# A mixture-of-experts block on one core: GpSimd's scatters in one run per round, results turned behind the third up step

## The chip, the cores and the metric

The kernel runs on one core of a Trainium2 chip. The metric is the device time of one execution in microseconds (us), the median of several runs. All tensors are float32 but for small bf16 tables of counts.

## The reference

The input is a batch of 8 images of 64 channels and 16 x 16 points, so 2048 tokens of 64 channels. First comes an attention over the 256 points of each image, then a feed-forward layer with 8 experts, of which each token uses the two with the largest logits.

```python
x = x + conv_attention(layernorm_over_channels(x))   # kq (32), v (32), softmax over 256 points, out (64)
t = tokens(x)                                        # 2048 x 64
n = layernorm(t)
gates = top2(softmax(n @ router_w.T)), renormalised  # 2 of 8 experts
h = silu(n @ w1[e].T) * (n @ w3[e].T)                # 682 hidden units
t = t + sum over the two experts of gate * (h @ w2[e].T)
```

## The kernel before

**First half.** The 2048 tokens lie as 16 tiles of 128. Two images (four tiles) are a pair, and the four pairs are worked through attention, layernorm and routing one after the other. Each token of a pair gets its two row numbers in a table `xs` in HBM, which holds a region of 2048 rows per expert. GpSimd writes the rows there by indirect DMAs: `scatter_row(p, at)` (from L354) sends one 128-row piece, `at` running over 4 tiles x 2 experts = 8 per pair, 32 in all. A row holds the 64 normalised channels and the number of its (token, expert) place.

**Second half.** The rows of the experts are cut into 39 pieces of 128 rows, which the code calls slots. Four slots are a round, so there are ten rounds (`NQ`), the last of three slots. Which expert a slot belongs to is computed on VectorE in three phases (after pair 1, pair 2 and pair 3), from which SyncE loads registers. The rows of rounds 0 and 1 need pairs 0 and 1, those of rounds 2 and 3 need pair 2, and those of rounds 4 to 9 need pair 3; SyncE waits for the scatters of these pairs (`landed(p)`, L299) ahead of `load_rows` (L292). `load_weights` (L276) loads the 565 KB of each slot's expert, with three rounds' worth of buffers. It waits for the down step of three rounds before.

A round i goes so:

- VectorE: `pair_up(i)` doubles the loaded rows (L781) and copies their place numbers to `y_row` (L786, L789). It stands on VectorE behind round i - 2.
- TensorE: `turn_x(i)` (L1013) transposes them into X_BANK, ScalarE's `columns(i)` (L496) copies them to `x_cols`.
- Six up steps s = 0 to 5. Step s of round i is number g = 6i + s. TensorE's `up(g)` makes 4 slots x 2 matmuls (L1031 with w1 in the upper half of the array, L1033 with w3 in the lower half); step 5 is the short tail (L1037). It signals `h1_done` and `h3_done`. ScalarE's `silu(g)` (L504, tail L508) and VectorE's `multiply(g)` (L827, tail L830) make the hidden units `hid`. TensorE may be one step ahead of silu and two ahead of multiply.
- TensorE's `down(i)` (L1059) multiplies `hid` by w2, 24 matmuls into one bank. ScalarE's `y_copy(i)` (L517) copies the result to SBUF, TensorE's `turn_y(i)` (L1073) transposes it back, VectorE's `results(i)` (L839) copies it to `y_out`, a ring of four rounds.
- GpSimd's `scatter_result(j)` (from L366) sends slot j's 128 rows of results by one indirect DMA to the table `ys` in HBM, in the order of (token, expert). It waits for `y_out_ready` at the first slot of a round.

TensorE's list of a round is up step 0, `turn_x(i+1)`, `turn_y(i-1)`, up steps 1 to 5, `down(i)`. VectorE's has `results(i-1)` behind `multiply` of step 0. No scheduler moves anything; each engine does its list in the order of the code, and the engines meet by semaphores.

**End.** When all results have landed, `ys` is read back in four parts, weighted by the gates, added to the tokens on TensorE, copied and stored.

GpSimd's own list, behind the tables of the start, is all row scatters, pair by pair, with the layernorm's inverse deviations in between, and then all result scatters:

```python
for p in range(PAIRS):
    for at in range(TPP * K_TOP):
        ...
        scatter_row(p, at)
...
for j in range(NS):
    scatter_result(j)
```

Of the kernel before, what the change touches and what calls it, by code (L numbers as in the profile page):

```python
# [16 lines left out]
K_TOP = 2  # L17
# [7 lines left out]
PAIRS = B // 2  # L25
TPP = 2 * TPB
# [5 lines left out]
QUAD = 4  # L32
CAP = B * N
NS = E + (K_TOP * CAP - 1) // SUB
NQ = -(-NS // QUAD)
# [16 lines left out]
STEPS = CHUNKS  # L52
# [9 lines left out]
def metaformer(nc, x_tok, projections, value_output, experts, xs, ys, out):  # L62
    with ExitStack() as ctx:
# [3 lines left out]
        def sem(name):  # L67
            return ctx.enter_context(nc.semaphore(name))
# [132 lines left out]
        h1_done, h3_done = sem("h1_done"), sem("h3_done")  # L201
# [124 lines left out]
        def _(pool):  # L326
# [38 lines left out]
            def scatter_result(j):  # L365
                i, h = divmod(j, QUAD)  # L366
                if h == 0:
                    pool.wait_ge(y_out_ready, i + 1)
                    pool.wait_ge(y_row_ready, i + 1)
                nc.gpsimd.indirect_dma_start(  # L370
                    ys, bass.IndirectOffsetOnAxis(ap=y_row[:, j:j + 1], axis=0),
                    y_out[:, i % RING, h, :], None).then_inc(y_scattered[i % RING], 16)
# [33 lines left out]
            pool.wait_ge(tables_made, TABLES)  # L406

            t_deviation(0)
            for p in range(PAIRS):
                for at in range(TPP * K_TOP):  # L410
                    if p == 0 and at == TPP * K_TOP - 2 or p == 2 and at == K_TOP:
                        t_deviation(p + 1)
                    scatter_row(p, at)
                if p == 1:
                    t_deviation(2)
            for j in range(NS):
                scatter_result(j)

        @block.scalar
# [128 lines left out]
        def _(dve):  # L548
# [306 lines left out]
            for i in range(NQ):  # L855
                for s in range(STEPS):
                    multiply(STEPS * i + s)
                    if s == 0 and i >= 1:
                        results(i - 1)
                    tables_between(i, s)  # L860
                if i + 2 < NQ:
                    pair_up(i + 2)
# [11 lines left out]
        def _(pe):  # L874
# [205 lines left out]
            for i in range(NQ):  # L1080
                for s in range(STEPS):
                    up(STEPS * i + s)
                    if s == (1 if i == 0 else 0) and i + 1 < NQ:
                        turn_x(i + 1)
                    if s == 0 and i >= 1:
                        turn_y(i - 1)
                down(i)
            turn_y(NQ - 1)
# [59 lines left out]
```

## Time and profile before

| what | value |
|---|---|
| timed runs | 174.99, 176.17, 176.45 us; median 176.17 |
| profiled execution, its span | 238.2 us |
| mean granted TensorE clock in it | 0.799 |
| TensorE busy (matmuls) | 166.9 us, 70% |
| VectorE busy | 99.7 us, 42% |
| GpSimd busy | 85.7 us, 36% |
| ScalarE busy | 70.8 us, 30% |
| result scatters on GpSimd (L370) | 39, 960 ns each |
| row scatters on GpSimd (L361) | 32, 987 ns each |
| first and last up step | from 68.5 us to 213.6 us of the span |

The profile is one execution that the hardware profiler recorded instruction by instruction; nothing of it lies outside the span of 238.2 us. That span is 62.0 us longer than the median of the timed runs, which are not recorded. Times in the rows are us from the start of the span. "Idle before" is how long the engine stood before an instruction, and the name behind the arrow is what ended that; "remote" is a release that the profile can't trace to an engine of this core, and "issue" stands where nothing that it shows was waited for.

### The profile page before, as it was taken

How to read it: one execution, taken by the hardware profiler on the slowest of the kernel's cores; microseconds unless marked ns; L12 is line 12 of the kernel's file. 1: busy time of each engine (PE TensorE's matmuls, PEld its weight loads, DVE VectorE, ACT ScalarE, POOL GpSimd, SP SyncE). 2: the span in 40 equal slices, each digit the busy share in tenths (PEclk: the TensorE clock that was granted, in tenths of full speed). 3: DMA queues.
4: the chain of work that ended last, by engine and by line, in shares of the span. 5: the costliest groups of instructions: out<-in, count | busy, mean ns of one | idle time of the engine just before them, and what ended most of it. 6: DMA issues, size and time to landing. Idle time of an engine off the chain costs nothing.

```text
span 238.2 us, 4880 instructions
## 1 busy us (share of the span) xinstructions
PE 166.9 (70%) x1682; PEld 139.1 (58%) x1682; DVE 99.7 (42%) x372; ACT 70.8 (30%) x141; POOL 85.7 (36%) x114
## 2 busy tenths in 40 slices
PE   3595957428683069589494994958949697895683
PEld 2364836307452068588393983948839597783543
DVE  2557568255583037584222433223232344342230
ACT  2377433013310034224232142222422323333101
POOL 2963577723277700603205033060230604142400
PEclk9999586555578559979799598895997979798579
DMA  6990000184570229652958075390661600000053
GB/s 185 322 297 20 11 25 22 31 267 151 159 290 23 50 81 328 216 210 46 364 169 313 3 240 196 88 346 4 203 228 42 266 10 14 11 15 11 17 176 91
DMA packets 19893, 33.00 MB, mean 139 GB/s; under 512 B 7691, under 2 KB 13100, under 8 KB 19868
## 3 DMA queue, kind: packets, MB, share of 16 engines
q1 hardware_dynamic: 16732, 29.55, 37.8%
q0 software_dynamic: 2272, 2.35, 3.0%
q10 hardware_dynamic: 864, 0.79, 1.0%
q8 instruction: 14, 0.23, 0.4%
q14 instruction: 11, 0.09, 0.1%
HBM read 25.55 MB, written 7.13 MB: 137 GB/s over the span
## 4 chain that ended last, share of the span: by engine, by line
issue 48%; POOL 21%; PE 11%; DVE 8%; DMA 3%; another core or an unknown queue 3%; ACT 3%; POOLq 1%; SPq 0%; ACTq 0%; DVEq 0%
POOL ys L370 15%; POOL xs L361 5%; PE psum L925 3%; PE psum L914 2%; ACT xn L426 2%; DMA y_in<-ys 2%; DVE rows L595 1%; PE psum L894 1%; PE psum L1103 1%; PE psum L885 1%; DMA ys<-y_out,y_row 1%; DMA proj<-projections 1%; DVE index L606 1%; DVE neg_max L584 1%
## 5 line engine op out<-in xcount | busy, mean ns | idle before, releaser
L370 POOL DMA_INDIRECT ys<-y_out,y_row x39 | 37.4, 960 | 104.0 <-DVE y_out L839 95.2
L827 DVE TENSOR_TENSOR hid<-psum,act_sb 128x512 f32<-128x512 f32 (+1 forms) x50 | 33.4, 676 | 88.9 <-ACT act_sb L504 61.6
L1031 PE MATMUL psum<-x_cols,weights 64*128 64x128 f32 x390 | 52.9, 286 | 13.9 <-issue 12.1
L1031 PEld LDWEIGHTS psum<-x_cols,weights 64*128 64x128 f32 x390 | 47.6, 193 | 19.4 <-issue 15.8
L1033 PE MATMUL psum<-x_cols,weights 64*128 64x128 f32 x390 | 53.1, 286 | 0.9 <-issue 0.9
L504 ACT ACTIVATE act_sb<-psum 128x512 f32<-128x512 f32 (+1 forms) x50 | 28.7, 586 | 70.0 <-remote 42.4
L1033 PEld LDWEIGHTS psum<-x_cols,weights 64*128 64x128 f32 x390 | 47.7, 193 | 1.1 <-issue 1.1
L1059 PE MATMUL psum<-hid,weights 128*64 128x128 f32 x468 | 42.8, 357 | 2.1 <-issue 1.1
L1059 PEld LDWEIGHTS psum<-hid,weights 128*64 128x64 f32 x468 | 39.3, 189 | 4.8 <-issue 2.7
L361 POOL DMA_INDIRECT xs<-xrows,pos x32 | 31.6, 987 | 12.9 <-issue 8.9
L1037 PE MATMUL psum<-x_cols,weights 64*106 64x128 f32 x78 | 8.7, 349 | 23.1 <-ACT act_sb L504 18.4
L1037 PEld LDWEIGHTS psum<-x_cols,weights 64*106 64x106 f32 x78 | 6.1, 208 | 24.7 <-ACT act_sb L504 19.6
L925 PE MATMUL psum<-u_sb,probsT 128*128 128x73 f32 x64 | 13.1, 373 | 5.2 <-issue 4.4
L925 PEld LDWEIGHTS psum<-u_sb,probsT 128*128 128x128 f32 x64 | 12.0, 281 | 7.6 <-issue 5.9
L517 ACT COPY y_cols<-psum 128x256 f32<-128x256 f32 (+1 forms) x10 | 3.6, 362 | 32.3 <-PE psum L1059 32.3
L957 PE MATMUL psum<-ones,before 128*128 128x512 bf16 x24 | 10.0, 562 | 1.8 <-issue 1.8
L452 ACT ACTIVATE probs<-psum,neg_max 128x256 f32<-128x256 f32 x16 | 6.7, 474 | 12.2 <-DVE neg_max L584 12.1
L460 ACT COPY probsT<-psum 128x512 f32<-128x512 f32 x8 | 4.7, 586 | 12.9 <-PE psum L914 8.5
L830 DVE TENSOR_TENSOR hid<-psum,act_sb 42x512 f32<-42x512 f32 x10 | 6.8, 682 | 3.5 <-ACT act_sb L508 3.5
L941 PE MATMUL psum<-taken,before 128*128 128x32 bf16 x4 | 0.7, 181 | 10.5 <-DVE taken L618 10.5
L914 PE MATMUL psum<-ident,probs 128*128 128x128 f32 x32 | 7.9, 395 | 0.3 <-ACT probs L452 0.3
L941 PEld LDWEIGHTS psum<-taken,before 128*128 128x128 bf16 x4 | 0.4, 99 | 13.1 <-issue 13.1
(148 smaller groups left out, 189.9 us busy)
## 6 DMA issues: line engine op xcount, KB each, us to landing
weights<-experts SPq DMA_DIRECT2D x39, 565.0 KB
xs<-zeros SPq DMA_DIRECT2D x4, 1040.0 KB, 11.1
x_in<-xs SPq DMA_DIRECT2D x39, 32.5 KB
ys<-y_out,y_row POOLq DMA_INDIRECT x39
xs<-xrows,pos POOLq DMA_INDIRECT x32
y_in<-ys ACTq DMA_DIRECT2D x2, 256.0 KB, 4.5
y_in<-ys SPq DMA_DIRECT2D x2, 256.0 KB, 4.3
x_sb<-x_tok SPq DMA_DIRECT2D x1, 384.0 KB, 3.4
```

Of the source, the lines that this page charges most:

```text
L361: nc.gpsimd.indirect_dma_start(xs, bass.IndirectOffsetOnAxis(ap=pos[:, p, at:at + 1], axis=0), xrows[:, TPP * p + at // K_TOP, at % K_TOP, ...
L370: nc.gpsimd.indirect_dma_start(ys, bass.IndirectOffsetOnAxis(ap=y_row[:, j:j + 1], axis=0), y_out[:, i % RING, h, :], None).then_inc(y_sca ...
L504: nc.scalar.activation(live(i, act_sb[:, g % 3, :]), live(i, H1_BANK[g % 2]), ACT.Silu).then_inc(silu_done, 1)
L827: nc.vector.tensor_tensor(live(i, hid[:, i % 2, s, :]), live(i, H3_BANK[g % 3]), live(i, act_sb[:, g % 3, :]), ALU.mult).then_inc(hid_done, 1)
L830: nc.vector.tensor_tensor(hid[0:TAIL, i % 2, s, :].rearrange("p (k n) -> p k n", k=2), TAIL_BANKS[0:TAIL], act_sb[0:TAIL, g % 3, :].rearra ...
L914: ins = nc.tensor.transpose(PT_BANK[:, N * j + P * i:N * j + P * (i + 1)], probs[:, b % 2, i, P * j:P * (j + 1)], ident[:])
L925: ins = nc.tensor.matmul(O_BANK[b % 2][:, (TX + 1) * i:(TX + 1) * (i + 1)], probsT[:, b % 2, j, P * i:P * (i + 1)], u_sb[:, 2 * b + j, E:] ...
L957: nc.tensor.matmul(bank[4], before[:], ones[:].unsqueeze(1).to_broadcast([P, BLK // P, P]), start=True, stop=True)
L1031: first_ = nc.tensor.matmul(H1_BANK[g % 2][:, src], weights[0:C, slot, P * s:P * (s + 1)], x_cols[0:C, i % 2, src], start=True, stop=True)
L1033: second_ = nc.tensor.matmul(H3_BANK[g % 3][:, src], weights[C:P, slot, P * s:P * (s + 1)], x_cols[C:P, i % 2, src], start=True, stop=True)
L1037: ins = nc.tensor.matmul(TAIL_BANKS[0:TAIL_W, h % 2, SUB * (h // 2):SUB * (h // 2 + 1)], weights[rows_, slot, TAIL_AT:TAIL_AT + TAIL_W], x ...
L1059: ins = nc.tensor.matmul(Y_BANK[C * (h % 2):C * (h % 2 + 1), P * (h // 2):P * (h // 2 + 1)], weights[:, slot, HP + C * s:HP + C * (s + 1)] ...
```

## The change

GpSimd's loop over the pairs ends before the last pair. The eight rows of the last pair and the results are sent inside a loop over the ten rounds. Round i begins with a wait until all six up steps of round i have been done by TensorE (`h3_done`); then five scatters go out in rounds 0 to 3 and four in each later round, rows of the last pair first. Round 0 so sends five rows, round 1 three rows and two results, rounds 2 and 3 five results each, and from round 4 on the four results of the round before. The three results of round 9 follow at the end.

On TensorE `turn_y(i-1)` and on VectorE `results(i-1)` move from behind step 0 to behind step 2 of round i.

```diff
             t_deviation(0)
-            for p in range(PAIRS):
+            for p in range(PAIRS - 1):
                 for at in range(TPP * K_TOP):
                     if p == 0 and at == TPP * K_TOP - 2 or p == 2 and at == K_TOP:
                         t_deviation(p + 1)
                     scatter_row(p, at)
                 if p == 1:
                     t_deviation(2)
-            for j in range(NS):
+
+            rows_sent, results_sent = 0, 0
+            for i in range(NQ):
+                pool.wait_ge(h3_done, STEPS * (i + 1))
+                for _ in range(5 if i < QUAD else 4):
+                    if rows_sent < TPP * K_TOP:
+                        scatter_row(PAIRS - 1, rows_sent)
+                        rows_sent += 1
+                    else:
+                        scatter_result(results_sent)
+                        results_sent += 1
+            for j in range(results_sent, NS):
                 scatter_result(j)
...
                     multiply(STEPS * i + s)
-                    if s == 0 and i >= 1:
+                    if s == 2 and i >= 1:
                         results(i - 1)
...
-                    if s == 0 and i >= 1:
+                    if s == 2 and i >= 1:
                         turn_y(i - 1)
```

GpSimd's list where the rows of the last pair (`xs<-xrows`) give way to the results (`ys<-y_out`), with the semaphores that each instruction waits for. Before:

```order
L361 DMA xs<-xrows,pos 16384x65 [waits pos_ready,tn_ready]
L361 DMA xs<-xrows,pos 16384x65
L361 DMA xs<-xrows,pos 16384x65 [waits tn_ready]
L361 DMA xs<-xrows,pos 16384x65
L361 DMA xs<-xrows,pos 16384x65 [waits tn_ready]
L361 DMA xs<-xrows,pos 16384x65
L361 DMA xs<-xrows,pos 16384x65 [waits tn_ready]
L361 DMA xs<-xrows,pos 16384x65
L370 DMA ys<-y_out,y_row 9088x64 [waits y_row_ready,y_out_ready]
L370 DMA ys<-y_out,y_row 9088x64 x3
```

And after the change:

```order
L361 DMA xs<-xrows,pos 16384x65 [waits pos_ready,tn_ready,h3_done]
L361 DMA xs<-xrows,pos 16384x65
L361 DMA xs<-xrows,pos 16384x65 [waits tn_ready]
L361 DMA xs<-xrows,pos 16384x65
L361 DMA xs<-xrows,pos 16384x65 [waits tn_ready]
L361 DMA xs<-xrows,pos 16384x65 [waits h3_done]
L361 DMA xs<-xrows,pos 16384x65 [waits tn_ready]
L361 DMA xs<-xrows,pos 16384x65
L370 DMA ys<-y_out,y_row 9088x64 [waits y_row_ready,y_out_ready]
L370 DMA ys<-y_out,y_row 9088x64
L370 DMA ys<-y_out,y_row 9088x64 [waits h3_done]
L370 DMA ys<-y_out,y_row 9088x64
```

The order of the scatters is the same; what is new are the waits for `h3_done`, one ahead of the first five and one for each later round.

VectorE's list around round 2, from the copy of pair_up that stands behind round 1 (`x_pairs`) to the one behind round 2. `hid` is multiply, `y_out` the copy of the results. Before:

```order
L781 COPY x_pairs<-x_in 128x512
L786 COPY y_row<-x_in 128x4
L827 TENSOR_TENSOR hid<-psum,act_sb 128x512
L839 COPY y_out<-psum 128x256
L827 TENSOR_TENSOR hid<-psum,act_sb 128x512 x4
L830 TENSOR_TENSOR hid<-psum,act_sb 42x512
L781 COPY x_pairs<-x_in 128x512
```

And after the change, whose lines from here on are numbered 11 higher:

```order
L792 COPY x_pairs<-x_in 128x512
L797 COPY y_row<-x_in 128x4
L838 TENSOR_TENSOR hid<-psum,act_sb 128x512 x3
L850 COPY y_out<-psum 128x256
L838 TENSOR_TENSOR hid<-psum,act_sb 128x512 x2
L841 TENSOR_TENSOR hid<-psum,act_sb 42x512
L792 COPY x_pairs<-x_in 128x512
```

The copy to `y_out` has moved from behind the first multiply to behind the third. TensorE's two transposes of `turn_y` move likewise; `turn_x` stays behind step 0.

## Rows read from the trace of the kernel before

**Rows 1.** waits of the whole kernel; us in total, times, longest:
```profile
ACT act_sb L504 <- remote: 42.4, 9, 14.4
...
DVE inv_sum L590 <- remote: 6.7, 1, 6.7
```

**Rows 2.** timeline of ScalarE; start, length, line, instruction, idle before and its end:
```profile
85.07 0.60 ACT L504 ACTIVATE act_sb<-psum 128x512 f32<-128x512 f32 x1 [14.45 <-remote]
...
140.34 0.60 ACT L504 ACTIVATE act_sb<-psum 128x512 f32<-128x512 f32 x1 [0.72 <-PE psum L1031]
...
141.70 0.60 ACT L504 ACTIVATE act_sb<-psum 128x512 f32<-128x512 f32 x1 [0.76 <-PE psum L1031]
...
146.15 1.08 ACT L504 ACTIVATE act_sb<-psum 128x512 f32<-128x512 f32 x2 [3.86 <-remote]
...
147.91 0.59 ACT L508 ACTIVATE act_sb<-psum 42x512 f32<-42x512 f32 x1 [0.67 <-PE psum L1037]
```

**Rows 3.** timeline of GpSimd, from round 0, round 3 and the end:
```profile
65.72 1.11 POOL L361 DMA_INDIRECT xs<-xrows,pos  x1 [0.20 <-issue]
...
71.00 0.96 POOL L361 DMA_INDIRECT xs<-xrows,pos  x1 [0.30 <-issue]
...
82.46 0.96 POOL L361 DMA_INDIRECT xs<-xrows,pos  x1 [0.30 <-issue]
...
140.37 0.96 POOL L370 DMA_INDIRECT ys<-y_out,y_row  x1 [10.96 <-DVE y_out L839]
...
144.17 0.96 POOL L370 DMA_INDIRECT ys<-y_out,y_row  x1 [0.30 <-issue]
...
221.36 0.96 POOL L370 DMA_INDIRECT ys<-y_out,y_row  x1 [5.32 <-DVE y_out L839]
```

**Rows 4.** timeline of VectorE:
```profile
71.22 0.42 DVE L781 COPY x_pairs<-x_in 128x512 f32<-128x512 f32 x1
...
85.88 0.69 DVE L827 TENSOR_TENSOR hid<-psum,act_sb 128x512 f32<-128x512 f32 x1 [12.55 <-remote]
...
119.31 0.41 DVE L781 COPY x_pairs<-x_in 128x512 f32<-128x512 f32 x1
...
139.68 0.41 DVE L839 COPY y_out<-psum 128x256 f32<-128x256 f32 x1
...
140.97 0.69 DVE L827 TENSOR_TENSOR hid<-psum,act_sb 128x512 f32<-128x512 f32 x1 [0.88 <-ACT act_sb L504]
...
217.76 0.68 DVE L830 TENSOR_TENSOR hid<-psum,act_sb 42x512 f32<-42x512 f32 x1 [1.11 <-ACT act_sb L508]
```

**Rows 5.** stretches: length, busy us (instructions) of PE, PEld, DVE, ACT, POOL, clock, DMA, GB/s:
```profile
140.40:145.10 4.70, 2.91 (x48) 2.53 (x44) 1.38 (x2) 1.13 (x2) 3.79 (x4) 1.00 0.97 350
...
198.60:203.40 4.80, 2.59 (x46) 2.39 (x42) 1.38 (x2) 1.55 (x3) 3.85 (x4) 1.00 0.07 24
...
65.70:74.50 8.80, 6.52 (x60) 4.61 (x58) 6.92 (x33) 1.18 (x2) 6.96 (x7) 0.84 0.51 195
74.50:83.40 8.90, 0.22 (x2) 0.03 (x1) 0.00 (x0) 0.00 (x0) 6.77 (x8) 0.55 0.16 41
```

**Rows 6.** the whole span in three stretches, columns as in rows 5:
```profile
0.00:85.00 85.00, 49.17 (x279) 35.12 (x279) 43.77 (x250) 24.96 (x56) 48.28 (x75) 0.72 0.42 130
85.00:221.00 136.00, 106.86 (x1333) 96.18 (x1335) 52.25 (x113) 43.86 (x80) 34.55 (x36) 0.85 0.43 149
221.00:238.20 17.20, 10.86 (x74) 7.75 (x70) 3.69 (x10) 1.96 (x6) 2.89 (x3) 0.77 0.34 98
```

**Rows 7.** timeline of SyncE's queue, two issues of four loads:
```profile
77.17 5.71 SPq L297 DMA_DIRECT2D x_in<-xs  x4
...
91.28 2.85 SPq L297 DMA_DIRECT2D x_in<-xs  x4
```

**Rows 8.** chain that ended last: the last scatter, from start to landing:
```profile
223.90 2.13 DMA ys<-y_out,y_row
```

**Rows 9.** line 1073: duration ns min/median/max, first and last start:
```profile
L1073 PE MATMUL psum<-ident,y_cols x20: 272/273/476, 94.2 to 220.3; 128*128 128x128 f32 x19, 64*128 64x64 f32 x1
```

## The prediction

> **What bounds the kernel now.** The first view to read is the list of waits. Its strangest line is ScalarE's: 42.4 us before its silu instructions, nine times, with no engine of this core named as the one it waited for [rows 1]. ScalarE's own timeline shows where [rows 2]. In round 3 the third silu starts at 141.70 after 0.76 us of idleness and takes 0.60; the fourth starts at 146.15 after 3.86, which is 3.1 more. In round 0 the gap is 14.45 us. GpSimd's timeline [rows 3] gives the pattern: in round 3 its four scatters run from 140.37 to 144.17 + 0.96 = 145.13, and ScalarE resumes 1.0 us after their end. The row scatters that began at 65.72 end at 82.46 + 0.96 = 83.42, and ScalarE resumes at 85.07, 1.65 us later. VectorE resumes at 85.88 after 12.55 us of idleness [rows 4]. TensorE stands too: two matmuls between 74.50 and 83.40 [rows 5]. So in the profiled execution every unbroken run of GpSimd scatters soon silences the three compute engines until it ends. That is what the change moves about, and the first question is whether the timed runs pay for it as well. Two views say mostly not.
>
> The first is a count of instructions [rows 5]. The stretch of the four scatters of round 3 holds 48 matmuls, 44 weight loads, 2 VectorE, 2 ScalarE and 4 GpSimd instructions: 100. That of round 8 holds 46 + 42 + 2 + 3 + 4 = 97. The DMA engines were 97% busy in the one and 7% in the other, so it isn't the traffic of the weights. In round 0, where fewer instructions start per us, the engines lasted from 65.70 to about 74.50, through 60 + 58 + 33 + 2 + 7 = 160 instructions, and then stopped. What fits all of them is a store of records that fills with instructions begun while GpSimd scatters, faster than it is emptied. That is a cost of being recorded, and a timed execution isn't recorded.
>
> On this the Trainium skill (NOTIFIC — the notification-queue block, section "7.1 Overflow: three behaviours, one of which stalls the engine") says that the block which writes trace records backpressures internally rather than lose one, and can so throttle an engine. The pattern of this trace agrees with it; no row shows the block itself.
>
> The second is a budget [rows 6]. TensorE is busy 106.86 us of the 136 us from 85 to 221, at a mean granted clock of 0.85; all of it at full clock would be 0.85 x 106.86 = 90.8. The stretch before is 85.0, less the silences of 12.55 [rows 4] and 6.7 us [rows 1] = 65.7; the stretch after is 17.2. The sum, with no stall and no idle TensorE in any round, is 65.7 + 90.8 + 17.2 = 173.7. The median of the timed runs is 176.17. So the timed runs have room for 2.5 us of stalls, where the recording shows about 12.5 + 9 x 3.1 = 40.4 from round 0 on. The bound isn't tight: if recording also stretches the small VectorE operations of the first 65.7 us, 10 us of stalls would fit. Without the stalls a round is bound by TensorE, which works through its own list almost without a gap.
>
> **The change, part by part.** Durations are from the profiled execution, whose span is 238.2 us; the median is 62.0 us below that, so terms that are stalls must not be carried over at full price.
>
> *The scatters of rounds 1 to 9, moved behind the tail up step.* None is added, only moved; one takes 1.27 us from start to start ((144.17 - 140.37) / 3, [rows 3]), four 5.06. Behind the tail step come silu and multiply of the tail and TensorE's down step. In the recording I expect the silence to shrink from about 3.1 us to 0.7 or less: the 48 matmul and 48 weight-load instructions of a down step reach the count of 100 only as the run ends. That makes 9 x 2.4 = 21.6 us of the recorded span. In the timed runs it is bounded by 0 and by the 2.5 us of the budget; I take half, -1.2.
>
> *The eight rows of the last pair, out of round 0.* In the recording the silence there goes, -12.5 us. So I expect a recorded span of 238.2 - 12.5 - 21.6 = 204. In the timed runs the stall is in the same -1.2. One real thing remains: the four x_in loads of SyncE in this stretch took 5.71 us to issue at 77.17, beside the scatters, against 2.85 at 91.28 with none [rows 7]. They feed pair_up(2), which stands on VectorE's queue ahead of round 1. The bounds are -2.9 (all of it on the path) and 0 (round 0's down step covers it, or the delay is recording too). I take 0, since both engines that would wait are themselves silent in this stretch, and keep -2.9 for the range.
>
> What then comes late: five rows go behind round 0's ups and three behind round 1's. The last lands about 2 x 1.27 + 2.13 = 4.7 us after the tail step, with the 2.13 us from start to landing of one scatter [rows 8]. SyncE waits for it ahead of quad 4's rows, and behind that wait stand the weights of quad 4 and everything later. But quad 4's weights wait for round 1's down step anyhow, and are needed two rounds later, while its rows are turned in round 3. Cost 0; it would cost only if the weights took most of two rounds to come.
>
> *Results turned and copied behind the third step.* TensorE's two transposes take 0.27 us each at either place [rows 9]: 0. VectorE's copy of 0.41 us [rows 4] leaves the gap after the first multiply and enters the one after the third. With no silence VectorE has 0.69 of multiply per step [rows 4] against 0.97 of TensorE's (2.91 us / 48 x 16 matmuls, [rows 5]), so one step of 1.10 runs 0.1 late, and the next has room: 0. If the room isn't there, it costs 0.41 a round, +3.7 in nine.
>
> *The end.* Quad 8's four results were sent long before the end and are now sent right ahead of quad 9's three. From the multiply of the last tail (217.76) to the first of the last three scatters (221.36) is 3.6 us [rows 3, 4]; ahead of it come the fifth silu and the tail's (0.6 each, [rows 2]) and some 0.2 of latency, so they are called for about 5.0 us after the tail step. The run of four ends at 5.06 + 0.2 = 5.3. GpSimd is late by 0.3: +0.3.
>
> *pair_up beside the scatters.* The copy of pair_up (f32, SBUF to SBUF) now always lies inside a run. At 71.22 one took 0.42 us inside the scatter that ran from 71.00 to 71.96 [rows 3, 4], where one away from any scatter takes 0.41 [rows 4]. So 0.
>
> The Trainium skill (SBUF — State Buffer, section "SBUF: two separate sides") has a rule against this: VectorE in a two-port mode and GpSimd take their shared port pair as an exclusive lock, and the second waits for the whole instruction. By it each copy would wait up to 0.96 us; the row at 71.22 disagrees.
>
> The sum for the timed runs: 176.17 - 1.2 + 0.3 = 175.3 us.
>
> **The rivals.** *First: a real part of the silence, or the x_in loads, is in the timed runs.* If recording stretches the first 65 us as well and a quarter of the 42 us are real, the change gives back a quarter of 12.5 + 21.6, or 8.5: 176.17 + 0.3 - 8.5 = 168.0. If only the loads are on the path: 175.3 - 2.9 = 172.4. For it speaks how clean the pattern is, and SyncE's slower issue; against it the budget. *Second, slower: VectorE's copy paces the middle steps.* The place is steps 3 and 4 of each of rounds 1 to 9, the price 0.41 each. In round 3 the third silu starts 1.36 us after the second [rows 2], not 0.97, so an engine other than TensorE may pace there, and the copy's old place, the gap after the first multiply, was free. In full: 176.17 + 3.7 + 0.3 = 180.2; half of the rounds: 178.3. It decides from about 0.2 us a round on. *Third: the change doesn't do what it says*, because the down step needs VectorE at once and is silenced like the up steps were. Then the recording shows the same 3.9 us gaps one phase later, and the timed run is where it was: 176.5.
>
> **How the numbers follow.** A measurement of this kernel can tell 1%, 1.76 us, from no change. The forecast of 175.3 has 0.41 and the third rival 0.06; of these 0.47, 0.04 each falls off either side of that 1%. The first rival 0.31: 0.20 at about 172.4 and 0.11 below 171. The second 0.22, of which 0.04 stays within 1%. Within 1%: 0.47 - 0.08 + 0.04 + 0.02 (loads half on the path) = 0.45; faster 0.31 + 0.04 - 0.02 = 0.33; slower 0.22 - 0.04 + 0.04 = 0.22. The range runs from 171.0 (loads, and the whole 2.5 of the budget: 176.17 + 0.3 - 2.9 - 2.5 = 171.1) to 178.6 (half of the copy rival and a little), and leaves out about 0.11 below and 0.08 above.
>
> **What would show it.** In the profile of the changed kernel: GpSimd's scatters start right behind the tail matmuls and are over before the next round's second silu; ScalarE's waits with no named engine fall from 42.4 us to under 12; the long gap of round 0 is gone; the span is near 204 while the median hardly moves. Were the silences real, the median would fall by 10 us or more along with the span. Were the copy to pace, the time from third to fourth silu would grow by 0.4 us with the scatters elsewhere.

## The result, and the profile after

| | before | after |
|---|---|---|
| median | 175.58 us (174.54 to 176.45, 4 runs) | 181.33 us (179.34 to 182.19, 4 runs) |
| ratio, 95% interval | 1 | 1.0285 (1.0189 to 1.038) |
| profiled execution: time, span | 238.2 us of span [rows 6] | 181.99 us, span 179.8 us |

The changed kernel is slower by 5.0 us at this ratio, where 175.3 us and no difference were forecast. Executions of a kernel come in two states some per cent apart: a ratio, here and below, compares fast runs alone, a median is over all of them, and an experiment without a ratio had too few fast ones. The time of a run was 1.7 to 3.0 us more than its span, so differences of either can be set side by side to about 1 us.

The list of waits of the kernel after (engine, line and what it waited for; us in total, times, the longest) has nothing left of ScalarE's 42.4 us for an unnamed engine [rows 1], and two kinds of wait that matter:

```profile
core 0 of [0], span 179.8 us
...
ACT act_sb L515 <- PE psum L1042: 29.4, 50, 3.3
...
DVE x_pairs L792 <- DMA x_in<-xs: 10.0, 6, 3.9
...
PE psum L1042 <- DMA weights<-experts: 2.5, 1, 2.5
```

ScalarE now waits for TensorE, 50 times; the 3.3 us is one place. VectorE's pair_up waits for rows, and TensorE once for weights. (A profile of before without silences, below, has the first of these two as well, 6.4 us in seven waits of at most 2.7, but not the second.) To see where, follow the chain of waits from round 0's first row scatter on (start, duration, work):

```profile
70.69 0.96 POOL xs L361
...
75.74 0.96 POOL xs L361
76.69 4.28 issue
81.21 1.10 POOL xs L361
82.61 0.96 POOL xs L361
83.87 7.34 DMA xs<-xrows,pos
91.91 0.63 SPq L297
97.56 8.54 DMA weights<-experts
```

Five of the last pair's rows are sent behind round 0's tail step and three behind round 1's. The last of the three starts at 83.87 and takes 7.34 us from start to landing. In the chain before, a scatter of results took 2.13 at the end of the kernel [rows 8]. Only then does SyncE issue quad 4's rows (a quad is the slots of one round), and behind them its weights, as its own timeline shows (here and below, what is in brackets is the idle time just before and what ended it):

```profile
start us, us, engine line op out<-in xcount [idle before <-releaser]
...
82.08 2.45 SPq L281 DMA_DIRECT2D weights<-experts  x4
91.38 2.20 SPq L297 DMA_DIRECT2D x_in<-xs  x4
96.00 1.91 SPq L281 DMA_DIRECT2D weights<-experts  x4
```

The issue of weights at 82.08 is what the late scatter stands behind: four loads of 565 KB, 2.26 MB. From then to the landing at 83.87 + 7.34 = 91.21 the DMA engines moved 266 GB/s, which is 2.43 MB, a little more than those weights:

```profile
core 0: us, PE busy (x) PEld busy (x) DVE busy (x) ACT busy (x) POOL busy (x), PEclk, DMA share, GB/s
82.08:91.21 9.13, 8.63 (x128) 7.34 (x126) 6.34 (x17) 3.94 (x7) 4.25 (x5) 1.00 0.79 266
```

Quad 4's weights have landed at 97.56 + 8.54 = 106.10. VectorE's pair_up and ScalarE's first silu of round 4 show who pays (the first two rows are VectorE's, for the rows of quads 4 and 5, the others ScalarE's of rounds 4 and 5):

```profile
95.19 0.43 DVE L792 COPY x_pairs<-x_in 128x512 f32<-128x512 f32 x1 [2.65 <-DMA x_in<-xs]
...
107.01 0.43 DVE L792 COPY x_pairs<-x_in 128x512 f32<-128x512 f32 x1 [3.87 <-DMA x_in<-xs]
```

```profile
107.61 0.60 ACT L515 ACTIVATE act_sb<-psum 128x512 f32<-128x512 f32 x1 [3.28 <-PE psum L1042]
...
116.90 0.60 ACT L515 ACTIVATE act_sb<-psum 128x512 f32<-128x512 f32 x1 [0.70 <-PE psum L1042]
...
118.58 0.60 ACT L515 ACTIVATE act_sb<-psum 128x512 f32<-128x512 f32 x1 [0.50 <-PE psum L1042]
119.47 0.60 ACT L515 ACTIVATE act_sb<-psum 128x512 f32<-128x512 f32 x1 [0.30 <-PE psum L1042]
120.93 0.60 ACT L515 ACTIVATE act_sb<-psum 128x512 f32<-128x512 f32 x1 [0.86 <-PE psum L1042]
121.82 0.60 ACT L515 ACTIVATE act_sb<-psum 128x512 f32<-128x512 f32 x1 [0.30 <-PE psum L1042]
...
125.09 0.37 ACT L528 COPY y_cols<-psum 128x256 f32<-128x256 f32 x1 [2.05 <-PE psum L1070]
```

Round 3 is longer by pair_up's first wait, for quad 4's rows, and round 4 by TensorE's wait for quad 4's weights. The second wait of pair_up cost nothing beyond that: it ended at 107.44, and TensorE came to turn these rows at 107.54.

ScalarE's copy of y, once a round, is a good clock for the rounds. In this profile it starts at 73.2, 84.6, 93.9, 104.0, 115.8 and 125.1, so rounds 1 to 5 take 11.4, 9.3, 10.1, 11.9 and 9.3 us, and 9.26 is what an undisturbed round takes from then to round 7. Against that, rounds 3 and 4 are 0.8 and 2.6 us too long: 3.4 us. Even 9.26 is more than it was, as the first experiment shows. The profile of before in front of the prediction can't serve here, since it has silences in every round.

### The profile page after: what moved, and what is told of

The parts are those of the page before. It is cut to its first block, busy times and chain, and to the rows that moved or that the text cites. A ratio compares the mean times of both kernels' runs of the same rounds, so it can differ in the third digit from the quotient of the medians.

```text
span 179.8 us, 4880 instructions
## 1 busy us (share of the span) xinstructions
PE 149.6 (83%) x1682; PEld 122.5 (68%) x1682; DVE 100.5 (56%) x372; ACT 71.4 (40%) x141; POOL 86.1 (48%) x114
## 4 chain that ended last, share of the span: by engine, by line
PE 54%; DMA 13%; issue 8%; DVE 7%; POOL 6%; ACT 5%; SPq 3%; POOLq 1%; DVEq 0%; ACTq 0%
PE psum L1042 18%; PE psum L1070 8%; PE psum L936 7%; DMA weights<-experts 5%; DMA xs<-xrows,pos 4%; POOL xs L361 4%; PE psum L925 3%; POOL ys L370 3%; PE psum L1114 2%; PE psum L1024 2%; DMA y_in<-ys 2%; PE psum L1048 2%; PE psum L905 2%; PE psum L896 2%; ACT xn L437 2%
## 5 line engine op out<-in xcount | busy, mean ns | idle before, releaser
L1042 PE MATMUL psum<-x_cols,weights 64*128 64x128 f32 x390 | 51.8, 282 | 2.8 <-DMA weights<-experts 2.5
L1042 PEld LDWEIGHTS psum<-x_cols,weights 64*128 64x128 f32 x390 | 46.3, 190 | 8.4 <-issue 7.2
L1044 PE MATMUL psum<-x_cols,weights 64*128 64x128 f32 x390 | 51.9, 282 | 0.0
L1044 PEld LDWEIGHTS psum<-x_cols,weights 64*128 64x128 f32 x390 | 46.2, 189 | 0.0
L1070 PE MATMUL psum<-hid,weights 128*64 128x128 f32 x468 | 28.8, 276 | 0.5 <-DVE hid L838 0.5
L1070 PEld LDWEIGHTS psum<-hid,weights 128*64 128x64 f32 x468 | 25.9, 137 | 2.3 <-DVE hid L838 0.7
L968 PE MATMUL psum<-ones,before 128*128 128x512 bf16 x24 | 11.3, 624 | 4.2 <-issue 4.2
L792 DVE COPY x_pairs<-x_in 128x512 f32<-128x512 f32 (+1 forms) x10 | 4.7, 472 | 10.0 <-DMA x_in<-xs 10.0
L968 PEld LDWEIGHTS psum<-ones,before 128*128 128x128 bf16 x24 | 3.0, 139 | 9.3 <-issue 9.3
L507 ACT COPY x_cols<-psum 128x512 f32<-128x512 f32 (+1 forms) x10 | 5.7, 574 | 8.2 <-PE psum L1024 8.2
L1024 PE MATMUL psum<-ident,x_pairs 128*128 128x128 f32 x39 | 6.9, 300 | 1.5 <-DVE x_pairs L792 1.5
L437 ACT ACTIVATE xn<-x_sb,shift_x,rstd 128x64 f32<-128x64 f32 x16 | 5.7, 429 | 5.3 <-DVE std L580 5.3
## 6 DMA issues: line engine op xcount, KB each, us to landing
xs<-zeros SPq DMA_DIRECT2D x4, 1040.0 KB, 11.9
```

The costliest lines, as they stand in the source:

```text
L437: ins = nc.scalar.activation(xn[:, p, i, m, :], x_sb[:, t, :], ACT.Identity, bias=shift_x[:, t:t + 1], scale=rstd[:, t:t + 1])
L968: nc.tensor.matmul(bank[4], before[:], ones[:].unsqueeze(1).to_broadcast([P, BLK // P, P]), start=True, stop=True)
L1024: ins = nc.tensor.transpose(X_BANK[:, P * h:P * (h + 1)], x_pairs[:, i % 2, h, :, :], ident[:])
L1042: first_ = nc.tensor.matmul(H1_BANK[g % 2][:, src], weights[0:C, slot, P * s:P * (s + 1)], x_cols[0:C, i % 2, src], start=True, stop=True)
L1044: second_ = nc.tensor.matmul(H3_BANK[g % 3][:, src], weights[C:P, slot, P * s:P * (s + 1)], x_cols[C:P, i % 2, src], start=True, stop=True)
L1070: ins = nc.tensor.matmul(Y_BANK[C * (h % 2):C * (h % 2 + 1), P * (h // 2):P * (h // 2 + 1)], weights[:, slot, HP + C * s:HP + C * (s + 1)] ...
```

## Experiments

Each was run beside the kernel before on the same chip, in three batches on three chips, so the medians of before differ (176.19, 177.09 and 175.62 us). The lengths of the rounds, from ScalarE's copies of y, stand in one table at the end of this section.

**The kernel before, profiled again** (no edit). The first profiled execution of it, 238.2 us, can't be compared with a timed one of 176; is that a trait?

> The kernel before, unchanged, profiled once more. Theory A (the 238.2 us of the first profiled execution, with its silences, belong to that one execution): a span of 172 to 176, rounds of about 8.97 us as in the kernel that only batches the results, ScalarE waiting for an unnamed engine for under 10 us in all. Rival B (this kernel, whose GpSimd scatters beside the up steps, is silenced whenever it is recorded): a span near 238 again, rounds of 14 to 16 us. Timed: the ratio holds 1.

Measured: 175.37 us (174.35 to 177.24), ratio 0.996 (0.9892 to 1.0029). The profiled execution took 176.11 us like the others. Its list of waits, for the same two lines of code as in [rows 1]:

```profile
core 0 of [0], span 174.4 us
...
DVE hid L827 <- ACT act_sb L504: 26.2, 42, 2.7
ACT act_sb L504 <- PE psum L1031: 25.3, 50, 2.2
```

Its scatters stand beside the up steps, as in the first profile: on GpSimd's timeline four start at 78.01, 79.28, 80.53 and 81.80, in round 1. No engine falls silent. VectorE's timeline has its multiplies all through them:

```profile
79.52 1.29 DVE L827 TENSOR_TENSOR hid<-psum,act_sb 128x512 f32<-128x512 f32 x2
...
82.37 0.68 DVE L827 TENSOR_TENSOR hid<-psum,act_sb 128x512 f32<-128x512 f32 x1
```

And ScalarE's timeline, in a middle round, gives the pattern that the changed kernel is to be compared with:

```profile
112.39 0.60 ACT L504 ACTIVATE act_sb<-psum 128x512 f32<-128x512 f32 x1 [0.70 <-PE psum L1031]
...
114.28 0.60 ACT L504 ACTIVATE act_sb<-psum 128x512 f32<-128x512 f32 x1 [0.72 <-PE psum L1031]
115.17 0.60 ACT L504 ACTIVATE act_sb<-psum 128x512 f32<-128x512 f32 x1 [0.30 <-PE psum L1031]
116.12 0.60 ACT L504 ACTIVATE act_sb<-psum 128x512 f32<-128x512 f32 x1 [0.35 <-PE psum L1031]
117.02 0.60 ACT L504 ACTIVATE act_sb<-psum 128x512 f32<-128x512 f32 x1 [0.30 <-PE psum L1031]
...
120.28 0.37 ACT L517 COPY y_cols<-psum 128x256 f32<-128x256 f32 x1 [2.05 <-PE psum L1059]
```

From silu to silu: 1.89, 0.89, 0.95, 0.90 us; after: 116.90 to 121.82 gives 1.68, 0.89, 1.46, 0.89. So the first gap gained 0.21 and the third lost 0.51: 0.30 more per round, 9.26 against 8.97 us. So theory A holds: the silences belong to one execution. What made them there isn't known. That recording is unlike the others in one more way: with the same 4880 instructions its trace holds 2608 updates of semaphores and 1739 landings of transfers, where those of the other kernels and of before, again hold 3500 to 3603 and 2575 to 2675. Something in the recording of that one execution may have gone wrong; no run here settles it.

**Only turn_y and results moved** (before, with the edit of the last two parts of the diff):

```diff
-                    if s == 0 and i >= 1:
+                    if s == 2 and i >= 1:
                         results(i - 1)
...
-                    if s == 0 and i >= 1:
+                    if s == 2 and i >= 1:
                         turn_y(i - 1)
```

> The kernel before, with one part of the change: turn_y and results stand behind step 2, GpSimd's list is the old one. Theory A (the break in TensorE's up steps costs): in the changed kernel silu 2 to silu 3 takes 1.46 us against 0.89 elsewhere, +0.57, and silu 0 to silu 1 takes 1.68 against 1.90 before, -0.22, so 0.35 a round and nine rounds: +3.1, timed 178.7. Theory B (all of the slowdown is GpSimd's new waits): no change, 175.6. Theory C (VectorE's copy paces): +0.41 x 9 = 3.7, and the third silu-to-silu gap is ended by VectorE, not TensorE. On the recording: if the silences during scatters are a cost of being recorded, this span is again near 238 us, 60 above its timed run.

Measured: 178.51 us (177.43 to 180.7) against 176.19, ratio 1.0189 (1.0092 to 1.0286). The middle rounds are 9.26 us, all of them. By the rounds the cost is less than that ratio: 0.29 in each of rounds 3 to 7, 0.4 in round 2, 0.3 in round 8 and nothing in rounds 1 and 9 come to about 2.2 us, 1.2%, which is within the interval. (That the median met the expected 178.7 is in part luck: 0.35 us in nine rounds was expected.) Its span was 175.7 us, not 238, with the scatters beside the up steps: the part of the expectation on the recording failed, which is what called for the run above.

**Which half of it costs.** First VectorE's part alone: `results` at s == 2, `turn_y` left at s == 0.

> Before, but VectorE alone copies the turned results behind the third step; TensorE's turn_y stays behind the first. Theory A (the 0.3 us a round belong to TensorE's broken run of up-step matmuls): rounds of 8.97 us as before, ratio 0.996 to 1.004. Rival B (VectorE's copy of 0.41 us between multiply 3 and 4 costs them): rounds of 9.26, ratio near 1.015.

Measured: 176.0 us (174.28 to 178.32, 12 runs) against 175.62, ratio 1.0008 (0.9961 to 1.0054); middle rounds 8.97. VectorE's copy is free at either place.

Then TensorE's: `turn_y` and `turn_x` together at the third step, with ScalarE's copy of x_cols (from round 1 on).

```diff
-                    if s == (1 if i == 0 else 0) and i + 1 < NQ:
+                    if s == (1 if i == 0 else 2) and i + 1 < NQ:
                         turn_x(i + 1)
-                    if s == 0 and i >= 1:
+                    if s == 2 and i >= 1:
                         turn_y(i - 1)
```

> Before with turn_y, results, and from round 1 on also turn_x and ScalarE's copy of x_cols, behind the third step: both kinds of transposes together again, but at the other place. Theory A (it is the second break in the run of matmuls that costs, 0.57 us where joined transposes cost 0.22): rounds of 8.9 to 9.05 us, ratio 0.995 to 1.005. Rival B (the third step has no room for them, wherever turn_x stands): 9.2 us or more a round, ratio 1.015 or more.

Measured: 175.4 us (174.03 to 177.94, 12 runs), ratio 0.9988 (0.9938 to 1.0038); middle rounds 8.97. So the third step has room, and it is the second break that costs. TensorE's timeline of the changed kernel shows how a break costs:

```profile
119.37 0.44 PE L1084 MATMUL psum<-ident,y_cols 128*128 128x128 f32 x2
119.74 0.37 PE L1042 MATMUL psum<-x_cols,weights 64*128 64x128 f32 x1
...
119.95 0.27 PE L1042 MATMUL psum<-x_cols,weights 64*128 64x128 f32 x1
...
120.06 0.27 PE L1042 MATMUL psum<-x_cols,weights 64*128 64x128 f32 x1
```

Within the run of up-step matmuls a pair (one with w1, one with w3) starts each 0.11 us (119.95 to 120.06), overlapping the one before. Around the two transposes it doesn't: from their start to the next pair are 0.37 us, and from that to the following pair 0.21. In the kernel with both together, turn_y's transposes start 0.49 us after the first of turn_x's, the next pair follows 0.32 us after them, and the break is made once:

```profile
113.38 0.66 PE L1013 MATMUL psum<-ident,x_pairs 128*128 128x128 f32 x4
113.87 0.38 PE L1073 MATMUL psum<-ident,y_cols 128*128 128x128 f32 x2
114.19 0.37 PE L1031 MATMUL psum<-x_cols,weights 64*128 64x128 f32 x1
```

**The other two parts of the change together** (the changed kernel with turn_y and results back at s == 0).

> The changed kernel with turn_y and results put back behind step 0, so GpSimd's part alone. Theory A: 181.3 - 3.1 = 178.2 timed, and the span falls from 179.8 to about 176.7. Theory B: 181.3, unchanged. What stays above 175.6 is the price of GpSimd's part: about 2.6, of which the wait of round 4 for weights (2.5 us before the first up step) should still be seen.

Measured: 179.15 us (177.95 to 181.62), ratio 1.0195 (1.0092 to 1.0297). Rounds 3 and 4 are 9.9 and 11.2 us. By these ratios the moved transposes are 0.9% of the change's 2.85%, but each has an interval of about 1% either way.

**The last pair's rows ahead of round 0 again** (`for p in range(PAIRS)` as before, results batched, turn_y at the third step).

> The changed kernel, but the eight rows of the last pair are sent ahead of round 0 as in the kernel before; four results per round behind the tail step, turn_y behind step 2. Theory A' (the late rows delay SyncE's queue: quad 4's rows and weights): the 2.5 us wait for weights ahead of round 4 and the 0.8 of round 3 go, -3.3, timed 178.0. Rival: the rows beside round 0 cost as much again in x_in loads or silences, 181.3. In the recording the silence of round 0 may come back (12 us of span) without the timed run moving.

Measured: 177.12 us (176.8 to 178.1), ratio 1.0114 (1.0042 to 1.0185). Rounds 3 and 4 are 9.26 us each. By the ratios the late rows are the other 1.7%, by the lengths of the rounds 3.4 us.

**Only the results batched** (before, rows ahead, turn_y at the first step, results behind the tail step).

> The kernel before with only the results held back to the tail step of each round (four at a time); rows and turn_y as before. If the three prices add up (turn_y 3.1, late rows 3.3, the end 0.6, sum 7.0 against 5.7 measured), this one costs only the 0.6 at the end: 176.2. If moving the results away from the up steps gives something back in the timed run (a real share of the silences), it is below 175.6, by up to 1.5: 174.5. If it is the batching that costs, it is 179 or more.

Measured: 176.18 us (174.59 to 177.66, 12 runs), ratio 1.0045 (0.999 to 1.01), which can't be told from no change. From the last copy of y to the issue of the last load (y_in) are 7.05 us, against 6.4 to 6.6 in the four kernels above that send results as they are ready.

**Only the rows late** (before, five behind round 0's tail step and three behind round 1's; results as ready).

> Before, but the eight rows of the last pair go behind the tail steps of round 0 (five) and round 1 (three); results and turn_y as before. Theory A (the third row behind round 1's tail lands some 7 us late behind the weights, so SyncE is late with quad 4's rows and weights, and round 4 waits): +3.0 to +3.4 us, ratio 1.017 to 1.02, with a round 3 or 4 longer than the others by 2 us or more and VectorE's pair_up waiting for x_in. Rival B (the late rows cost only together with results in the same run of scatters): ratio within 0.997 to 1.006 and all middle rounds near 9.0 us.

Measured: 181.53 us (178.03 to 183.26) against 177.09; no ratio, but the lowest of each are 178.03 and 174.33, 3.7 us apart. Rounds 4 and 5 are 12.0 and 10.0 us, and in both TensorE waits for weights, 3.9 us in all. So results in the same run of scatters aren't needed for it, and B falls; the size, 4.3 us by the rounds of this one profile, is above A's, though the timed runs are too few to say so.

**All eight rows behind round 0's tail step** (the changed kernel otherwise):

```diff
-                for _ in range(5 if i < QUAD else 4):
+                for _ in range(TPP * K_TOP if i == 0 else 4):
```

> The changed kernel, but all eight rows of the last pair go behind round 0's tail step (in place of five there and three behind round 1's). Theory A (the rows cost because the last three leave behind round 1's tail, into a queue full of weights): they have landed by 83, the longer rounds 3 and 4 are gone, all middle rounds are 9.26; time as with the rows ahead of round 0, 177 to 178, ratio 1.009 to 1.014. Rival B (any row behind round 0's up steps makes quad 4 late): a round of 11 us or more and a ratio above 1.02.

Measured: 177.76 us (176.89 to 179.67), ratio 1.013 (1.0048 to 1.0212). The last row starts at 80.08 on GpSimd's timeline, ahead of the weights that SyncE issues at 82.58. SyncE issues quad 4's rows at 88.10, not 91.38, and its weights at 92.64, not 96.00:

```profile
82.58 2.66 SPq L281 DMA_DIRECT2D weights<-experts  x4
88.10 2.13 SPq L297 DMA_DIRECT2D x_in<-xs  x4
92.64 1.88 SPq L281 DMA_DIRECT2D weights<-experts  x4
```

All middle rounds take 9.26 us. The landing of the rows isn't in this trace, but all else is as theory A had it: the rows may wait for round 0, but not for the next batch of weights.

**No wait in the last round** (the changed kernel, but GpSimd's `wait_ge(h3_done, ...)` left out for i = 9).

> The changed kernel, but in the last round GpSimd's wait for the tail step is left out, so that quad 8's results go as soon as they are in SBUF; the last three follow when they are ready. Theory A (at the end the last three results stand behind quad 8's four): the time from the last copy of y to the issue of the last load falls from 7.05 to about 6.4 us, so -0.66 us, ratio 1.025 against the kernel before (changed kernel 1.0285). Rival B (the end is set by ScalarE and TensorE, the extra is chance): 7.0 us there again and the ratio of the changed kernel.

Measured: 181.89 us (179.1 to 182.43), ratio 1.0273 (1.0158 to 1.0388). The end is 6.4 us, as A had it. The ratio fell by 0.0012 where 0.0035 was expected, and the interval is too wide to tell either from nothing. In its profiled execution (182.43 us, the longest of its six runs) round 4 took 13.2 us, the longest of all. The windows of 1 us in it (first us, then PE, PEld, DVE, ACT, POOL with their instructions, the granted clock, DMA):

```profile
105.00:106.00 1.00, 0.00 (x0) 0.00 (x0) 0.00 (x0) 0.09 (x1) 0.70 (x1) 1.00 0.30 95
...
108.00:109.00 1.00, 1.00 (x6) 0.71 (x4) 0.30 (x1) 0.60 (x1) 0.22 (x1) 0.51 1.06 411
109.00:110.00 1.00, 1.00 (x9) 0.95 (x10) 0.39 (x1) 0.59 (x1) 0.00 (x0) 0.50 1.02 362
...
112.00:113.00 1.00, 1.00 (x14) 0.71 (x14) 0.60 (x2) 0.60 (x1) 0.00 (x0) 1.00 0.98 369
```

TensorE stood idle from about 104.7 to 106.9, worked for about 1.1 us at full clock, and from 108 to about 111.5 it was granted half of its clock, the lower of its two levels (1.2 GHz). Over round 4 of the changed kernel, TensorE's idle stretch was 2.53 us, against 2.24 here, and the clock stayed at 1.00. So in this execution the wait cost a second time through the clock. It is one observation, and no difference between kernels rests on it.

**The change without its three costs** (all eight rows behind round 0's tail, turn_y and results at the first step, no wait in the last round).

> The changed kernel with its three costs taken out: all eight rows behind round 0's tail step, turn_y and results back behind the first step, no wait of GpSimd for the last tail step. What is left of the change is that scatters stand behind the tail steps and not beside the up steps. Theory A (the scatters cost nothing beside the up steps in a run that is not silenced, so nothing is gained): rounds of 8.97 us, 6.4 us at the end, ratio 0.996 to 1.004. Rival B (a part of the silences of the 238 us execution is in each timed run, so moving the scatters gains once the costs are out): ratio 0.99 or less.

Measured: 175.96 us (174.58 to 178.2, 12 runs), ratio 1.0011 (0.9962 to 1.0061), middle rounds 8.97. Taking the scatters from beside the up steps gives nothing that an interval of 0.5% either way can tell; theory A holds.

**A try at something faster.** Round 1, which has three blocks of table work between its steps, takes 11.3 us in the kernel before, 2.3 more than the others. Here the first block's operations go one or two to a step and the other two go behind pair_up.

> Before, but VectorE's tables of the third pair, which stand in three blocks between the steps of round 1, are spread one or two operations to a step, and the last two blocks go behind that round's pair_up. Theory A (round 1 takes 11.3 us where others take 9.0 because silu and multiply of its steps stand behind those blocks): round 1 falls to 9.5 or less and the time by 1.5 to 2.3 us, ratio 0.987 to 0.992. Rival B (the rows of the last pair then leave later and quad 4's loads are late): round 1 is shorter but a round 3 or 4 grows by as much, ratio 0.997 to 1.01.

Measured: 179.23 us (176.23 to 180.7), ratio 1.0028 (0.9923 to 1.0132). Round 1 fell to 9.4 us and round 2 rose to 10.8: the two blocks now stand on VectorE's queue ahead of round 2's first multiply, from 83.64 to 86.56 in its timeline, behind a pair_up that itself waited for rows until 83.22. So they were moved, not hidden: B's ratio, but not by its cause, since it is the very next round that grows. Rounds 4 and 7 are 10.3 and 10.6 us as well, in this one execution: around them TensorE waits 1.2 and 0.7 us for weights and pair_up 2.6 and 3.5 us for rows.

| kernel | rounds 1 to 9, us | end: y copied to y_in issued |
|---|---|---|
| before, again | 11.3, 9.0, 9.0, 9.0, 9.0, 9.0, 9.9, 8.9, 7.6 | 6.4 |
| changed | 11.4, 9.3, 10.1, 11.9, 9.3, 9.3, 9.3, 9.2, 7.6 | 7.1 |
| turn_y and results moved | 11.3, 9.4, 9.3, 9.3, 9.3, 9.3, 9.3, 9.2, 7.6 | 6.4 |
| results alone moved | 11.6, 9.1, 9.0, 9.0, 9.0, 9.0, 9.0, 8.9, 7.6 | 6.6 |
| all turns at the third step | 10.4, 9.2, 9.0, 9.1, 9.0, 9.0, 9.0, 8.9, 7.6 | 6.4 |
| results batched | 11.3, 9.0, 9.0, 9.0, 9.0, 9.1, 9.0, 8.9, 7.6 | 7.1 |
| changed, turn_y back | 11.4, 9.0, 9.9, 11.2, 9.3, 9.1, 9.9, 8.9, 7.6 | 7.0 |
| changed, rows ahead | 11.3, 9.3, 9.3, 9.3, 9.3, 9.3, 9.3, 9.2, 7.6 | 7.1 |
| only rows late | 11.4, 9.0, 9.2, 12.0, 10.0, 9.0, 9.0, 8.9, 7.6 | 6.4 |
| changed, rows behind round 0 | 11.4, 9.3, 9.3, 9.3, 9.3, 9.3, 9.3, 9.2, 7.6 | 7.1 |
| changed, last round free | 11.4, 9.3, 9.6, 13.2, 9.3, 9.3, 9.3, 9.2, 7.6 | 6.4 |
| tables spread | 9.4, 10.8, 9.0, 10.3, 9.0, 9.0, 10.6, 8.9, 7.6 | 6.4 |
| without the three costs | 11.5, 9.0, 9.0, 9.0, 9.0, 9.4, 9.0, 8.9, 7.6 | 6.4 |

The 9.9 of before, again in round 7 is the same kind of wait in small: its pair_up waits 2.7 us for rows there. So the loads are close behind TensorE even where no row leaves late, and a single long round in one profile is no proof of a change.

## Why the prediction was wrong

*The silences as "a cost of being recorded".* This step failed in its reading and was harmless in its number. Five profiles with GpSimd's scatters where they were before (before, again; turn_y and results moved; results alone moved; all turns at the third step; tables spread) have no wait for an unnamed engine, in spans of 172.1 to 177.0 us. So recording alone doesn't make the silences, and a count of instructions [rows 5] can't be the whole reason either: all these programs have the same 4880. The span forecast for the changed kernel, 204 us, became 179.8. That the pattern agreed with the rule of the Trainium skill on the block that writes trace records (NOTIFIC — the notification-queue block, section "7.1 Overflow: three behaviours, one of which stalls the engine") was no proof of it: the same scatters are in all these traces. What that leaves is a fault of recording in one execution, for which the smaller number of its semaphore updates speaks and which nothing here shows. The budget from busy time and clock [rows 6] did its work: it said 173.7 us for an execution without stalls, and the recorded one took 174.4. The -1.2 us that I took for stalls (0.7%) wasn't there: the ratio with the three costs out is 1.0011 (0.9962 to 1.0061). The harm was elsewhere: with 40 us of silence in the trace, the real rhythm of a round couldn't be read, and terms of 0.3 us a round and a few us of late loads were argued from rows that the silences had deformed.

*"Cost 0; it would cost only if the weights took most of two rounds to come."* This is the step that failed most: 3.4 us in rounds 3 and 4, 1.7% by the ratios. Two of its premises were wrong. The last row was to land 4.7 us after the tail step. It landed at 91.21, 10.0 us after round 1's first scatter at 81.21, because the 2.13 us from start to landing was read where the queues were almost empty, at the end [rows 8], and here the scatter left behind 2.26 MB of weights: 7.34. (It took 6.27 in the profile of the kernel with turn_y put back, and 6.24 in that without the last wait.) And "needed two rounds later" took the waits for quad 4 as all independent. The condition that I named was the wrong one. From the first issue at 96.00 to the last landing at 106.10 the weights took 10.1 us, about one round and not two, and that was enough: their issue stood behind rows that were themselves 3.3 us later than with all eight behind round 0 (91.38 against 88.10), and TensorE, done with round 3 at 103.9, could have used them 2.5 us before it began at 106.45. What the step lacked is the slack that these weights had. In before, again they were issued at

```profile
91.43 1.88 SPq L281 DMA_DIRECT2D weights<-experts  x4
```

and the DMA engines were done with the burst by about 100 (235 GB/s from 99 to 100, 50 from 100 to 101), while TensorE began round 4 at 102.22. That leaves about 2 us, by an estimate from these rows, for an issue that now came 4.6 us later. The silences had stretched rounds 1 to 8 to 13 to 16 us in the profile that I had, and hidden how small this slack is.

*"TensorE's two transposes take 0.27 us each at either place: 0."* This failed too. Their own time is nearly the same (a median of 0.30 us in the changed kernel, 0.27 in before, again); that of what surrounds them isn't. [Rows 9] give the durations of the transposes and nothing of the gaps around them. Behind turn_x they joined a break that was there anyway; behind the third step they made a second one. From one silu to the next this is -0.21 and +0.51, so 0.29 to 0.30 a round in the seven rounds that show it, and 2.2 us in all. The ratios put it at 1.9% by itself and at 0.9% within the change; with their intervals of about 1% either way they agree with each other and with the 1.2% of the rounds. That the break is the cause is shown (1.0189 with it, 0.9988 with all turns together); what TensorE does in it isn't.

*VectorE's copy: 0.* Right, shown by its own run (1.0008). The second rival priced the slower outcome nearly right, 180.2 us, but that is luck, by the wrong engine: it had 0.41 a round for VectorE at steps 3 and 4. The time between the third and the fourth silu grew as it said, but VectorE's share in that is nothing.

*The end: +0.3.* Right in kind, mis-sized: 0.66 us. On VectorE's timeline of the changed kernel y_out is ready at 161.44 + 0.36 = 161.80, and a scatter follows its copy by 0.27 us (before, again: 157.00 to 157.27), so the last three were called for at 162.07. The first started at 162.73, right behind quad 8's four:

```profile
157.68 0.96 POOL L370 DMA_INDIRECT ys<-y_out,y_row  x1 [2.67 <-PE psum L1048]
...
161.46 0.96 POOL L370 DMA_INDIRECT ys<-y_out,y_row  x1 [0.30 <-issue]
162.73 0.96 POOL L370 DMA_INDIRECT ys<-y_out,y_row  x1 [0.30 <-issue]
```

I had them called for 5.0 us after the tail step. Taken from 157.4, 0.3 ahead of the first scatter, it was 4.7, and the first of the last three started at 5.3, as I had worked out for the end of the four. The term that was too long is that of the two silus, added one after another at 0.6 us each. In this round of three slots the fifth takes 0.49, and it is under way (157.04 to 157.53) while TensorE still works on the tail (156.92 to 157.60).

*pair_up beside the scatters: 0.* Nearly right. Of its six copies between 70 and 125 in the changed kernel, all of them beside a scatter, four took 0.42 or 0.43 us (that of 95.19 wholly inside the scatter from 95.16 to 96.12) and two took 0.64 and 0.56; no round shows it. By the lock of the Trainium skill that the prediction weighed (SBUF — State Buffer, section "SBUF: two separate sides") a copy could wait up to the 0.96 us of a scatter; the longest here is 0.22 over the usual 0.42.

*The x_in loads, -2.9 us kept in the range.* Nothing of it was there: before, again issues the same four in 1.89 us at 69.00, with scatters running.

By the profiles the parts add up: 2.2 for the transposes, 3.4 for the late rows and 0.65 at the end are some 6.2 us, and from the end of round 1 to the load of y_in the changed kernel takes 82.8 us where the one with only the results batched, less its 0.65 at the end, takes 76.8. The ratio says 5.0 us, with an interval from 3.3 to 6.7. What stays open is what silenced the engines in the first profile of before, and why the wait in round 4 differs from run to run (2.3, 2.6, 3.0 and 3.9 us over a normal round in four profiles, the last with the lower clock).

## What to carry to other kernels

If a profiled execution takes a third longer than the timed ones, as here, profile the same kernel again before anything is read from it. For a transfer that is moved later, take the time to landing from a place with the same traffic, see which bulk load it now stands behind, follow what is issued after it in order, and compare the delay with the slack of that work (here some 2 us). In this kernel a pair of transposes amid matmuls of another shape cost TensorE the break that it made, and nothing where it joined one; so try keeping such instructions together, and price a move from the start of the neighbour before to the second neighbour after.

## What the runs showed of the hardware

- A scatter of rows that GpSimd sent took 7.34 us from start to landing when SyncE had begun to issue 2.26 MB of weights 1.8 us earlier, against 2.13 us for a scatter of results at the end of the kernel, where little else is under way. In two more profiles it took 6.2 and 6.3 us.
- Two 128x128 transposes between 64-row matmuls that otherwise start in pairs each 0.11 us lengthened the sequence of silus by 0.51 us, and by 0.21 where they followed four other transposes.
- After 2.24 us of idleness in the middle of the kernel and about 1.1 us of work, TensorE was granted half of its clock (1.2 GHz) for some 3.5 us in one execution (of the kernel without the wait in the last round); it kept the full clock (2.4 GHz) after 2.53 us of idleness in another (the changed kernel).
- VectorE's copy from SBUF to SBUF (float32, 128x512) took 0.43 us wholly inside a scatter instruction of GpSimd (95.16 to 96.12), against 0.41 away from one [rows 4]; the longest of six beside scatters took 0.64.
- One execution of a kernel showed its compute engines silent through every run of GpSimd scatters, 238.2 us in all; another of the same code took 174.4 us of span with none.
